# Expert weights loaded into the place of their low halves, all inputs resident, variances seven tiles ahead and scales in the next step

## What is computed

```python
xn = _layernorm(x)
# attention: heads of width 8, keys and queries interleaved in Wqk
qk = (xn @ Wqk_w.T + Wqk_b).reshape(b, n, H, E, 2); v = xn @ Wv_w.T + Wv_b
attn = softmax(q @ k.T) / HEAD_DIM ** 0.5
a = (attn @ v).reshape(b, n, H * E) @ Wo_w.T + Wo_b
# experts
logits = xn @ W_gate + b_gate
_, top_idx = jax.lax.top_k(logits, 2)
y = relu(einsum('bsd,edh->bseh', xn, W_e) + b_e)
f = take_along_axis(y, top_idx).mean(axis=2)
out = x + a + f
```

## Time and profile before

| | us |
|---|---|
| time, 3 runs | 364.0, 361.82, 358.92 (median 361.82) |
| the profiled execution | 363.15 |
| its span, first to last instruction | 361.4 |
| busy in the span: PE, DVE, POOL, ACT | 309.9, 230.7, 200.9, 174.2 |
| mean granted TensorE clock, share of full speed | 0.927 |

### The profile page before, as it was taken

One profiled execution on the slowest core, in us unless ns is written; L12 is line 12 of the kernel. 1 busy time (PEld: TensorE's weight loads), 2 busy tenths in 40 slices (PEclk: granted clock), 3 DMA queues, 4 the chain that ended last, 5 costly groups with the idle time before them and its releaser, 6 DMA issues.

```text
span 361.4 us, 5494 instructions
## 1 busy us (share of the span) xinstructions
PE 309.9 (86%) x1629; PEld 222.8 (62%) x1629; DVE 230.7 (64%) x498; ACT 174.2 (48%) x311; POOL 200.9 (56%) x179
## 2 busy tenths in 40 slices
PE   2785976175999999999999899399999999999973
PEld 1574976174888888888888688154546645544421
DVE  4767767871343444766767864967786977884313
ACT  1658775041234333332323243456777677677650
POOL 3366899208686866666565723847388887100000
PEclk9989689555999999999999999769999999999999
DMA  7899975505245445564444511349999999510113
GB/s 206 306 407 378 273 242 166 233 0 170 92 150 172 146 146 176 163 217 147 153 139 150 134 67 60 116 127 172 308 241 183 213 188 142 118 61 0 58 60 117
DMA packets 31004, 59.60 MB, mean 165 GB/s; under 512 B 5504, under 2 KB 5632, under 8 KB 30848
## 3 DMA queue, kind: packets, MB, share of 16 engines
q1 hardware_dynamic: 20864, 39.59, 31.3%
q0 software_dynamic: 7728, 18.62, 25.0%
q10 hardware_dynamic: 2384, 1.04, 1.1%
HBM read 38.52 MB, written 18.61 MB: 158 GB/s over the span
## 4 chain that ended last, share of the span: by engine, by line
PE 83%; issue 6%; DVE 4%; ACT 4%; ACTq 2%; DMA 1%; DVEq 0%; POOLq 0%
PE ps_s L1114 30%; PE ps_t L1051 11%; PE ps_o L1066 9%; PE ps_s L980 8%; PE ps_s L1040 7%; PE ps_t L1094 5%; PE ps_m L1011 3%; PE ps_t L966 2%; PE ps_s L1084 2%; ACT probs L664 2%; PE ps_m L1015 1%; PE ps_o L1040 1%; DMA row_in<-xn_rows,gather_i 1%; PE ps_m L1023 1%; PE ps_m L1024 1%
## 5 line engine op out<-in xcount | busy, mean ns | idle before, releaser
L1114 PE MATMUL ps_s<-w_split,t_hi 128*128 x312 | 101.1, 405 | 2.0 <-issue 2.0
L664 ACT ACTIVATE probs<-ps_t 128x512 f32<-128x512 f32 x128 | 69.7, 597 | 34.6 <-PE ps_t L1051 29.6
L846 DVE TENSOR_REDUCE row_max<-ps_s 128x1 f32<-128x512 f32 x112 | 72.3, 684 | 15.6 <-PE ps_s L1040 10.1
L490 POOL TENSOR_TENSOR row_mid<-row_mid,bias_o 128x512 f32<-128x512 f32 x39 | 50.8, 1302 | 43.8 <-ACT row_mid L611 43.8
L611 ACT ACTIVATE row_mid<-row_mid 128x512 f32<-128x512 f32 x39 | 24.7, 633 | 92.8 <-DVE row_mid L867 80.3
L1114 PEld LDWEIGHTS ps_s<-w_split,t_hi 128*128 128x128 f32 x312 | 56.4, 191 | 13.0 <-issue 2.7
L1114 PE MATMUL ps_s<-w_split,t_lo 128*128 x156 | 61.7, 396 | 0.0
L1051 PE MATMUL ps_t<-q_t,k_head 128*128 128x512 f32 x128 | 57.2, 458 | 3.1 <-ACT probs L664 2.7
L521 POOL DMA_INDIRECT acc<-expert_rows,slots_i x32 | 49.7, 1552 | 16.0 <-issue 8.4
L1051 PEld LDWEIGHTS ps_t<-q_t,k_head 128*128 128x128 f32 x128 | 23.9, 191 | 44.3 <-ACT probs L664 29.7
L471 POOL DMA_INDIRECT row_in<-xn_rows,gather_i x39 | 37.9, 972 | 22.1 <-DVE gather_i L824 15.8
(11 more groups left out here) (133 smaller groups left out, 412.8 us busy)
## 6 DMA issues: line engine op xcount, KB each, us to landing
expert_rows<-row_mid SPq DMA_DIRECT2D x39, 256.0 KB, 2.0
stage<-in_L_ffn_W_e_dram SPq DMA_DIRECT2D x16, 512.0 KB, 7.0
xn_rows<-row_mid SPq DMA_DIRECT2D x16, 256.0 KB, 5.3
acc<-in_L_attn_x_dram SPq DMA_DIRECT2D x16, 256.0 KB, 3.8
out_dram<-res SPq DMA_DIRECT2D x16, 256.0 KB
row_in<-in_L_attn_x_dram SPq DMA_DIRECT2D x8, 256.0 KB, 6.3
w_split<-in_L_attn_x_dram SPq DMA_DIRECT2D x8, 256.0 KB, 8.6
bias_e<-in_L_ffn_b_e_dram SPq DMA_DIRECT2D x1, 2048.0 KB, 7.7
```

What stands on the lines that cost most here:

```text
L490: pool.tensor_tensor(row_mid[:, n % 4, :], row_mid[:, n % 4, :], bias_o[:], ALU.add).then_inc(y_done, 1)
L664: act.activation(probs[:, n % 2, j, :], ps_t[:, j % 2, :], ACT.Exp).then_inc(exp_done, 1)
L846: dve.tensor_reduce(row_max[:, b % 2, h, i:i + 1], score_bank(n), AX.X, ALU.max).then_inc(max_done, 1)
L1114: mm = pe.matmul(ps_s[:, n % 2, :], a[:, n % 2, ks], rhs, start=(k == 0), stop=(k == 3 * KC - 1))
```

## The change

- Expert halves are loaded straight into the place of their own low half, w_split[.., 1, ..]; ACT reads them from there into the high half, and POOL subtracts in place. The ring `stage` and all its waits are gone. A load waits for nothing now but its turn in SP's list: half i+3 is issued in step i, halves 0 to 2 ahead of step 0.
- x tiles 6 to 15 lie in `x_far` (20 KB in each partition, where `stage` was). Ten x tiles are issued ahead of step 0, tile i+10 in step i; no x load waits for a place.
- The loads of Wo (two) and of the output bias move from ACT's list to SP's, behind the store of xn(0).
- SP's load of bias_e no longer waits for the splits of the expert weights.
- DVE: `moments` run seven tiles ahead (5, 6, 7 in step 0), and scales(2), (3), (4) stand right behind low(1), low(5), low(9), a step after their variance instead of at the end of the same step.
- POOL: ROOT_AT becomes {2: 2, 6: 3, 10: 4}.
- Two semaphores of the accumulation at the end become one with a count of 32.

```diff
-RW = 5
-RX = 14
-ROOT_AT = {1: 2, 4: 3, 8: 4}
+XF = 10
+WF = 3
+ROOT_AT = {2: 2, 6: 3, 10: 4}
...
-        stage = sb("stage", [P, RW, 2, F], F32, sub)
+        x_far = sb("x_far", [P, NT - RI, D], F32, sub)
...
+        def load_w(queue, c):
+            e, half = divmod(c, 2)
+            src = we[e].rearrange("(c p) h -> p c h", p=P)[:, 2 * half:2 * half + 2, :]
+            queue.dma_start(w_half(c, 1).bitcast(F32), src).then_inc(w_in[c], 16)
...
             def load_x(i):
-                if i >= RX:
-                    sp.wait_ge(xn_made, i - RX + 1)
-                sp.dma_start(x_buf(i), x_rows[i * P:(i + 1) * P, :]).then_inc(x_in[i % RX], 16)
-            def load_w(c):
-                if c >= RW:
-                    sp.wait_ge(w_lo_made, c - RW + 1)
...
+                sp.dma_start(x_buf(i), x_rows[i * P:(i + 1) * P, :]).then_inc(x_in[i], 16)
...
+                if i == 0:
+                    sp.dma_start(wo_dst[:, :, 0:HD], wo_src).then_inc(wo_in, 16)
+                    sp.dma_start(wo_dst[:, :, HD:2 * HD], wo_src).then_inc(wo_in, 16)
+                    sp.dma_start(bias_o[:], bo.rearrange("(a d) -> a d", a=1).to_broadcast([P, D])).then_inc(bias_o_in, 16)
-                if i + RI + 2 < NT:
-                    load_x(i + RI + 2)
-                if i + 2 < NT:
-                    load_w(i + 2)
+                if i + XF < NT:
+                    load_x(i + XF)
+                if i + WF < 2 * NE:
+                    load_w(sp, i + WF)
...
-                pool.wait_ge(w_in[c % RW], 16 * (c // RW + 1))
+                pool.wait_ge(w_in[c], 16)
                 pool.wait_ge(w_hi_made, c + 1)
-                pool.tensor_tensor(w_split[:, e, 1, cs, :], stage[:, c % RW, :, :], w_split[:, e, 0, cs, :].bitcast(F32),
+                pool.tensor_tensor(w_half(c, 1), w_half(c, 1).bitcast(F32), w_half(c, 0).bitcast(F32),
                                    ALU.subtract).then_inc(w_lo_made, 1)
...
-            ahead = {0: (5, 6), 1: (7,)}
             for i in range(NT):
                 low(i)
-                for k in ahead.get(i, (i + 6,)):
+                if i in (1, 5, 9):
+                    scales(i // 4 + 2)
+                for k in (5, 6, 7) if i == 0 else (i + 7,):
                     if k < NT:
                         moments(k)
                         if k % 4 == 3:
...
-                for k in ahead.get(i, (i + 6,)):
-                    if k < NT and k % 4 == 3:
-                        scales(k // 4 + 1)
```

More of the change, by code:

```diff
@@ L181, in attention_and_experts @@
         weights_split = sem("weights_split")
-        x_in = [sem(f"x_in{s}") for s in range(RX)]
+        x_in = [sem(f"x_in{i}") for i in range(NT)]
         xn_out = [sem(f"xn_out{s}") for s in range(4)]
@@ L192, in attention_and_experts @@
         proj_kept = sem("proj_kept")
-        w_in = [sem(f"w_in{s}") for s in range(RW)]
+        w_in = [sem(f"w_in{c}") for c in range(2 * NE)]
         w_hi_made = sem("w_hi_made")
@@ L231, in attention_and_experts @@
         acc_in = [sem(f"acc_in{i}") for i in range(NT)]
-        ya_in = [sem(f"ya_in{i}") for i in range(NT)]
-        yb_in = [sem(f"yb_in{i}") for i in range(NT)]
+        y_in = [sem(f"y_in{i}") for i in range(NT)]
         y_relu = sem("y_relu")
@@ L293, in x_buf, with w_half @@
         def x_buf(i):
-            at = i % RX
-            if at < RI:
-                return row_in[:, at, :]
-            return w_split[:, NE - 1, (at - RI) // KC, (at - RI) % KC, :].bitcast(F32)
-        def x_landed(eng, i):
-            eng.wait_ge(x_in[i % RX], 16 * (i // RX + 1))
+            return row_in[:, i, :] if i < RI else x_far[:, i - RI, :]
+        def w_half(c, part):
+            e, half = divmod(c, 2)
+            return w_split[:, e, part, 2 * half:2 * half + 2, :]
+        def load_w(queue, c):
+            e, half = divmod(c, 2)
+            src = we[e].rearrange("(c p) h -> p c h", p=P)[:, 2 * half:2 * half + 2, :]
+            queue.dma_start(w_half(c, 1).bitcast(F32), src).then_inc(w_in[c], 16)
         def weight_buf(n):
@@ L329, in load_x @@
             def load_x(i):
-                if i >= RX:
-                    sp.wait_ge(xn_made, i - RX + 1)
-                sp.dma_start(x_buf(i), x_rows[i * P:(i + 1) * P, :]).then_inc(x_in[i % RX], 16)
-            def load_w(c):
-                if c >= RW:
-                    sp.wait_ge(w_lo_made, c - RW + 1)
-                e, half = divmod(c, 2)
-                src = we[e].rearrange("(c p) h -> p c h", p=P)[:, 2 * half:2 * half + 2, :]
-                sp.dma_start(stage[:, c % RW, :, :], src).then_inc(w_in[c % RW], 16)
+                sp.dma_start(x_buf(i), x_rows[i * P:(i + 1) * P, :]).then_inc(x_in[i], 16)
             for i in range(RI):
                 load_x(i)
-            load_w(0)
+            load_w(sp, 0)
             load_x(RI)
-            load_w(1)
-            load_x(RI + 1)
+            load_w(sp, 1)
+            for i in range(RI + 1, XF):
+                load_x(i)
+            load_w(sp, 2)
+            wo_src = wo.rearrange("(c p) k -> p c k", p=P)
+            wo_dst = weight_buf(2).rearrange("p (c k) -> p c k", c=KC)
             for i in range(NT):
@@ L516, in _, with add_rows @@
                 pool.wait_ge(y_out[s], 16 * ((NS - s + 3) // 4))
-            def add_rows(i, r, before_it, landed):
-                pool.wait_ge(before_it[i], 16)
+            def add_rows(i, r, earlier):
+                pool.wait_ge(earlier[i], 16)
                 pool.indirect_dma_start(acc[:, i, :], None, y_dram,
                                         bass.IndirectOffsetOnAxis(ap=slots_i[:, r, i:i + 1], axis=0),
-                                        compute_op=ALU.add).then_inc(landed[i], 16)
+                                        compute_op=ALU.add).then_inc(y_in[i], 16)
             for i in range(NT + 2):
                 if i < NT:
-                    add_rows(i, 0, acc_in, ya_in)
+                    add_rows(i, 0, acc_in)
                 if i >= 2:
-                    add_rows(i - 2, 1, ya_in, yb_in)
+                    add_rows(i - 2, 1, y_in)
                 if i == NT // 2:
@@ L544, in _ @@
             act.dma_start(bias_p[:, 3 * HD:PW], row(bg)).then_inc(biases_in, 16)
-            wo_src = wo.rearrange("(c p) k -> p c k", p=P)
-            wo_dst = weight_buf(2).rearrange("p (c k) -> p c k", c=KC)
-            act.dma_start(wo_dst[:, :, 0:HD], wo_src).then_inc(wo_in, 16)
-            act.dma_start(wo_dst[:, :, HD:2 * HD], wo_src).then_inc(wo_in, 16)
-            act.dma_start(bias_o[:], row(bo)).then_inc(bias_o_in, 16)
             act.wait_ge(consts_ready, 2)
@@ L553, in split_w @@
             def split_w(c):
-                e, half = divmod(c, 2)
-                act.wait_ge(w_in[c % RW], 16 * (c // RW + 1))
-                act.activation(w_split[:, e, 0, 2 * half:2 * half + 2, :], stage[:, c % RW, :, :],
-                               ACT.Copy).then_inc(w_hi_made, 1)
+                act.wait_ge(w_in[c], 16)
+                act.activation(w_half(c, 0), w_half(c, 1).bitcast(F32), ACT.Copy).then_inc(w_hi_made, 1)
             def hi(i):
```

10 lines of the change are left out of this document (3 added, 7 removed).

## The result

The changed kernel takes 370.78 us (median of 4 runs, 369.45 to 371.2) against 360.37 (358.13 to 364.0) for the one before: ratio 1.0277, 95% interval 1.0218 to 1.0337. It is slower. The medians lie 10.4 us apart, the spans of the two profiled executions 7.5 (368.9 against 361.4), since the profiled execution of the kernel before is one of its slow ones (363.15 us, 2.8 over the median) and that of the changed kernel isn't (370.64). The two traces account for the 7.5; what they leave out is taken up at the run with POOL's last split held back.

The account below looks back on a forecast made before the run. Stage 1's handovers between engines, ending with tile 15, were taken as the bound, no engine being full. Adding 2.8 + 2.5 + 2.3 gave 370.8 from the profiled execution, 369.4 from the 361.8 median; forecast 370.0 us, range 364.5 to 374.0.

Parts of the forecast that it names:

- The circle: Stage 1, steps 1, 5, 9: after hi(i), ACT's split, POOL's split, root and DVE's scales run in a row; +7.6 us.
- Its three prices: Delays forecast for stage 1's steps with scales: step 1 +2.8 us, step 5 +2.5, step 9 +2.3.
- Wo's detour: Stage 1: Wo's transposes behind project(2) hold ACT, so low(4) waited 2.64 us for hi(4); forecast to stay.
- The steps between: Stage 1's eleven steps without scales: taken as 0 us, with -3 as low end and +3 as high end.
- the clock: Rival: longer low-clock stretches after stage 1's stalls add 3 us, in-order stores some more; 373 to 374; over 372: 0.15.
- The loads at nothing: Stage 1's loads without waits and resident x: 0 us on the path, bounds 0 and -1.9.
- My sum for the first store: SP's queue in stage 1: 4.0 MB ahead of the first store, 10.1 us at 397 GB/s; no cost to norm(4).
- It has 14.7 us to spare and doesn't set the end: POOL's expert-weight splits in stage 1 end at 65.15, wanted only by gather_i at 79.82, so not setting the end.
- The sum of 7.6: Stage 1's three steps with scales together, 2.8 + 2.5 + 2.3 us, the whole slowdown summed for the change.
- The rival of the other side, only gains left: Stage 1's roots are ready when DVE reaches scales, leaving gains of 2.8 and 1.9 us: 357 to 359; chance 0.05.
- What the profile would show: Three DVE waits for POOL's root about 4 us each, low(5) to low(6) 6.5, keep_proj(15) near 68, stages 2 to 4 unchanged.

Follow-up runs that it names:

- the run with POOL's last split held back: Kernel before, with POOL's last split (half 15) waiting until DVE's mask is made: 358.85 against 361.19 us, ratio 0.9950.
- the table put back: Changed kernel with only POOL's ROOT_AT back at {1: 2, 4: 3, 8: 4}: 359.81 against 361.19 us, ratio 0.9961.
- the order alone: Kernel before with only DVE's order of moments and scales and POOL's ROOT_AT changed, loads untouched: 369.43 us, ratio 1.0264.
- the loads alone: Changed kernel with DVE's order and POOL's ROOT_AT put back, only the load changes kept: 361.36 against 361.19 us, ratio 1.0016.

## Why the prediction was right, and where its steps were off

- **The circle.** Its three prices were 2.8, 2.5 and 2.3. Measured from the two timelines: low(2) is 23.90 - 21.06 = 2.84 late, step 5 takes 6.74 instead of 4.00 (+2.74), step 9 takes 6.36 instead of 4.00 (+2.36). That it is this and not the loads is shown by the table put back (0.9961), by the order alone (1.0264) and by the loads alone (1.0016). Step 9 is the circle as I had drawn it. In step 5 POOL's backlog from Wo's detour held the root 0.4 us longer than ACT's split did, and I had no term for it.
- **The steps between.** I took 0 with 3 either way. Against the trace before they cost 1.1: low(2) to low(5) 10.24 for 9.93, low(6) to low(9) 8.21 for 8.39, low(10) to low(15) 11.35 for 10.40. Together low(15) is 9.0 late and not 7.6. But the trace that I started from had half clock in just these steps. Against the execution with the same first stage in which low(15) starts at 54.24 they cost 4.3, more than my high end. I had named the clock as what may cost more there, and that was right: behind the stalls of steps 5 and 9 it took 3.8 us, by the run with the table put back. The term was mis-sized, not the mechanism.
- **The loads at nothing.** Right. ACT's wait for half 2 shrank, as allowed, and norm(4) waited 1.9 us for scales(2) instead. My sum for the first store took ten tiles and three halves as 4.0 MB; they are 4.2, which makes 10.6 us of the 10.1. Nothing hangs on it: ACT doesn't wait for a store in stage 1 of the changed kernel.
- **"It has 14.7 us to spare and doesn't set the end".** This step is wrong. POOL's splits don't hold gather_i, but they hold DVE's pick by the shared port, 17 us earlier in the program. I read who waits by semaphore and not how long an instruction takes. The row was there to be read: pick 2.50 us beside 0.42 for an instruction of the same shape in the same stage. In the kernel before this hid 2.6 us of tile 15's lateness, and so the wrong step and the underestimate of the steps between nearly cancelled: 9.0 - 2.6 = 6.4 at gather_i, for 7.6.
- **The total, 370.0 for 370.78.** That it came so close is in part luck. The sum of 7.6 stands against 10.4 between the medians, and I had set it on 361.8, where the median of four runs is 360.37, and added 0.6 for the clock. The direction and the three waits are not luck.
- **The rival of the other side, only gains left.** It put 357 to 359 on roots that are ready. With the table put back the time was 359.8, as the shared port holds the routing to POOL's end; with POOL's last two splits moved to DVE as well, 355.7 to 357.6.
- **What the profile would show.** The three waits were to be about 4 us, the first perhaps 4.5; they were 2.96, 3.77 and 4.16, the first shorter because low(1) itself came 1.0 later behind moments(7), whose tile DVE waited for. Keep_proj(15) was to be at about 68 and stands at 69.19. Low(5) to low(6) was to be 6.5 and is 6.74. Stages 2 to 4 were to be as long as before, but the routing is 2.6 us shorter (17.02 against 19.65 from keep_proj(15) to gather_i), as it no longer stands beside POOL's splits.

## What to carry to other kernels

Before moving a step in one engine's list, follow its wait through the lists of the others, instruction by instruction: if it leads back to something that is started only by the instruction just ahead of it, the wait has a fixed price, here 5.6 us from hi(9)'s end to the scales' end (6.0 in step 5), whatever else is early. What stands behind the waiting instruction pays too, so put it ahead (worth 3.7 us of low(15) here). Before taking one trace as the base of a sum, ask what the clock did in it: the same first stage ended 3.5 us apart in two executions. And an engine with time to spare can still hold another by a port: look for one instruction with two durations, and give the engine that shares the port nothing to do while the path crosses.
